# Attention in a fused four-layer kernel: Q and K normalised by two operations, the heads of Q transposed while K is made

## The reference

```
q = (layernorm(x) @ Wq).reshape(B, Sq, H, D)      # H = 16 heads, D = 128
k = (ctx @ Wk).reshape(B, Skv, H, D)
v = (ctx @ Wv).reshape(B, Skv, H, D)
q = q * rsqrt(mean(q*q, axis=-1) + eps) * gq      # per token and head
k = k * rsqrt(mean(k*k, axis=-1) + eps) * gk
attn = softmax(einsum('bqhd,bkhd->bhqk', q, k) / sqrt(D))
x = x + einsum('bhqk,bkhd->bqhd', attn, v).reshape(B, Sq, H*D) @ Wo
```

## Time and profile before

| | us |
|---|---|
| runs | 832.14, 829.62, 832.06 |
| median | 832.06 |
| the profiled execution | 832.21 |
| its span (first to last instruction) | 830.3 |
| attention's first and last step, about | 311 to 604 |

### The profile page before, as it was taken

The page is one execution under the profiler, slowest core; times in us unless marked ns, Lnnn a source line. Parts: engine busy times, 40 slices in busy tenths (PEclk is TensorE's granted clock), DMA queues, the critical chain, the costliest instruction groups (busy, mean ns, idle before and its releaser), DMA issues. The chain is left out here.

```text
span 830.3 us, 12112 instructions
## 1 busy us (share of the span) xinstructions
PE 758.1 (91%) x4322; PEld 624.7 (75%) x4322; DVE 544.8 (66%) x930; ACT 432.4 (52%) x879; POOL 383.8 (46%) x311
## 2 busy tenths in 40 slices
PE   7566766999999989999999999999799999999997
PEld 2222222888888878889889898888678888888886
DVE  6999998743433567878888887887865333333333
ACT  3876652334433346666676676667553433333432
POOL 0699874336755543223322322332233655555552
PEclk9699999999999999999999999999999999999999
DMA  4613000111446101101101020000000434342431
GB/s 138 255 52 139 19 19 1 39 39 34 143 141 195 42 1 39 39 1 40 37 3 39 2 77 1 2 1 20 20 20 22 159 100 124 93 129 91 132 96 51
DMA packets 23262, 53.88 MB, mean 65 GB/s; under 512 B 4057, under 2 KB 6690, under 8 KB 22178
## 3 DMA queue, kind: packets, MB, share of 16 engines
q1 hardware_dynamic: 23040, 52.96, 20.0%
q10 hardware_dynamic: 162, 0.14, 0.0%
HBM read 51.87 MB, written 1.21 MB: 64 GB/s over the span
## 5 line engine op out<-in xcount | busy, mean ns | idle before, releaser
L1163 POOL TENSOR_TENSOR f_h_lo<-f_hid,f_h_hi 128x512 fp32r<-128x512 f32 x84 | 108.8, 1295 | 128.2 <-ACT f_h_hi L1138 127.7
L1254 DVE TENSOR_TENSOR f_su<-f_sg,psum 128x512 f32<-128x512 f32 x72 | 49.5, 687 | 168.4 <-PE psum L111 150.9
L1138 ACT ACTIVATE f_h_hi<-f_hid 128x512 fp32r<-128x512 f32 x84 | 53.1, 632 | 164.0 <-DVE f_hid L1271 145.2
L109 PE MATMUL psum<-xT_hi,w_ring 128*128 128x512 f32 x336 | 133.8, 398 | 1.9 <-ACT f_cT L1129 0.7
L110 PE MATMUL psum<-xT_lo,w_ring 128*128 128x512 f32 x336 | 132.9, 396 | 0.0
L111 PE MATMUL psum<-xT_hi,w_ring 128*128 128x512 f32 x336 | 132.8, 395 | 0.0
L109 PE MATMUL psum<-w_ring,f_h_hi 128*128 128x256 f32 x336 | 95.3, 284 | 1.9 <-POOL f_h_lo L1163 1.2
L1657 POOL TENSOR_TENSOR a_rr<-a_ss,eps 128x8 f32<-128x8 f32 x32 | 6.5, 203 | 194.1 <-DVE a_ss L1696 194.1
L111 PE MATMUL psum<-w_ring,f_h_lo 128*128 128x256 f32 x336 | 94.5, 281 | 0.0
L110 PE MATMUL psum<-w_ring,f_h_hi 128*128 128x256 f32 x336 | 94.2, 280 | 0.0
L1568 ACT ACTIVATE a_p_exp<-psum,a_nmax 128x256 f32<-128x256 f32 x128 | 59.5, 470 | 57.5 <-DVE a_nmax L1711 57.5
(11 more groups left out here) (217 smaller groups left out, 1852.6 us busy)
## 6 DMA issues: line engine op xcount, KB each, us to landing
w_raw<-in_moe SPq DMA_DIRECT2D x42, 384.0 KB, 3.3
m_b_all<-b_rows SPq DMA_DIRECT2D x8, 1024.0 KB, 4.6
f_comb<-scratch SPq DMA_DIRECT2D x60, 128.0 KB, 3.4
a_raw<-in_w_pair SPq DMA_DIRECT2D x8, 768.0 KB, 4.3
f_comb<-scratch SPq DMA_DIRECT2D x12, 224.0 KB, 3.5
f_comb<-scratch SPq DMA_DIRECT2D x12, 192.0 KB, 3.6
f_comb<-scratch SPq DMA_DIRECT2D x12, 160.0 KB, 3.4
f_comb<-scratch SPq DMA_DIRECT2D x12, 96.0 KB, 3.5
```

What stands on the lines that cost most here:

```text
L109: pe.matmul(out, a[0], b[0], start=first, stop=False, skip_group_check=True)
L1138: act.activation(h_hi[:, j % HS, :], hid[:, j % HS, :], ACT.Copy).then_inc(mix.h_hi_s, 1)
L1163: pool.tensor_tensor(h_lo[:, j % HS, :], hid[:, j % HS, :], h_hi[:, j % HS, :], ALU.subtract)\
```

## The change

`normed` becomes two DVE operations of 512 columns each, Q first and then K, and each raises `qkn_s`. `heads_turned` waits ahead of the four transposes of Q for the first and ahead of those of K for the second. The waits that stood ahead of the calls go, and POOL's wait on the same semaphore counts in twos. The amount of work is the same.

```diff
                 def heads_turned(n):
 
                     for which, dst in enumerate((QT, KT)):
+                        pe.wait_ge(qkn_s, 2 * n + which + 1)
                         for hh in range(HP):
                             for tile in range(2):
...
                     if not (static and t >= NUA - 1):
-                        pe.wait_ge(qkn_s, t + 2)
                         heads_turned(n + 1)
...
                     norm_turned(pe, sh, s, 1, h, out)
-                pe.wait_ge(qkn_s, 1)
                 heads_turned(0)
...
                     if not (isinstance(t, int) and t < 2):
-                        pool.wait_ge(qkn_s, t - 1)
+                        pool.wait_ge(qkn_s, 2 * (t - 1))
                     pool.tensor_tensor(rr[:, n % 2, :], ss[:, n % 2, :], sh.eps[:, :], ALU.add).then_inc(mse_s, 1)
...
-                    dve.tensor_tensor(qkn[:, n % 2, :].rearrange("p (a f) -> p a f", f=HD),
-                                      qk_banks(t).rearrange("p (a f) -> p a f", f=HD),
-                                      rr[:, n % 2, :].unsqueeze(2).to_broadcast([P, 8, HD]), ALU.mult).then_inc(qkn_s, 1)
+                    for at in range(2):
+                        dve.tensor_tensor(qkn[:, n % 2, at * UW:(at + 1) * UW].rearrange("p (a f) -> p a f", f=HD),
+                                          qk_banks(t)[:, at * UW:(at + 1) * UW].rearrange("p (a f) -> p a f", f=HD),
+                                          rr[:, n % 2, 4 * at:4 * at + 4].unsqueeze(2).to_broadcast([P, 4, HD]), ALU.mult)\
+                            .then_inc(qkn_s, 1)
```

## The result

| | before | after |
|---|---|---|
| runs, us | 832.14, 829.62, 832.06, 832.50 | 826.12, 824.65, 824.31, 823.06 |
| median, us | 832.10 | 824.48 |
| ratio (95% interval) | | 0.9911 (0.9891 to 0.9931) |
| profiled execution, us | 832.21 | 826.12 |
| its span, us | 830.3 | 824.2 |

What follows compares the result with a forecast made beforehand. The prediction took the ring, 8.95 us per step, to bound the kernel. Its terms, 7.3 + 0.4 - 0.1 = 7.6 us of gain, gave 824.5 us (chance 0.80), range 821 to 828.5.

Steps and rivals of the forecast that it cites:

- the ring: Attention loop from projection through squares, sums, roots, `normed` and transposes to the next projection; 8.95 us, sets the step.
- The two halves: In `normed`: Q ready at R + 0.74, K at R + 1.34; before, both at R + 1.28.
- R: Start of `normed` in a step, the zero point from which times in us are counted.
- The transposes: PE hands over to the projection at R + 1.80, before R + 2.13: 0.33 us saved, step 8.62.
- Where it counts: Of 23 stalls in the attention, 22 gain 0.33 us each, 7.3 us; the last has no projection behind it.
- The first unit: Start of the attention, transposes partly at the low clock: 0.4 us of gain, bounds 0 and 0.7.
- The last unit: End of the attention, where the 0.06 us of longer `normed` shows: 0.1 us of loss.
- the fold steps: Seven attention steps in which PE also folds weights; PE comes to K's transposes after K is ready: no gain.
- What stands behind: Behind the longer `normed`: ACT keeps 0.23 us of cover ahead of `squares`, DVE 0.8 us idle ahead of the sums.
- other wait: Rival: another wait in the attention takes the place, leaving 3.3 us of gain, 829 us; chance 0.10.
- the halves weren't dear: Denies the rival that `normed` halves cost more: at 1.02 us each, a slower kernel, 841 us; chance 0.04.
- the clock: Rival: more PE work falls into the second low-clock stretch, in the router's products: 826.2 or 827.9 us; chance 0.06.

Runs made afterwards that it cites:

- one wait: The changed kernel, but the transposes of Q wait for both `normed` operations; ratio 1.0035 to the kernel before.
- K in two parts: The changed kernel with K's half of `normed` split again by token tile, K's transposes waiting tile by tile; ratio 0.9864 to the kernel before.
- the second profile: The changed kernel measured once more with no further edit; ratio 0.9913 to the kernel before.

## Why the prediction was right

*What bounds the kernel.* Right: the ring. It was shortened (the change), lengthened by 0.15 us on GpSimd and shortened by 0.07 us on VectorE, and the step followed by 0.38, 0.16 and 0.07 us.

*The two halves.* 681 ns each and 0.60 apart, as taken from the low parts of the probabilities: the spread operand costs nothing in four blocks either. K was there at R + 1.34, as worked out. The fixed price that the Trainium skill (VectorE: DVE Perf Modes, section on the TRN2 errata) gives would have made it 0.125 us later than the whole, not 0.06; here the measurement decides. That each operation has a price is right in kind: by itself the split made the kernel slower. The section's advice, though, is tiles of 512 elements or more, and both halves are that; it speaks against this split less than the prediction has it.

*The transposes.* Q's start was right. The hand-over was at R + 1.75, not R + 1.80: four transposes and the restart take 0.41 us, not 0.46. The restart's price, read from eight transposes that wait once, is hardly paid a second time. That made the step 8.57 instead of 8.62, and the gain of a step 0.38 instead of 0.33 us.

*Where it counts.* Twenty-two steps were too many by two. The steps behind the first unit took 8.93 and 8.84 us instead of 8.94 and 8.94, a gain of 0.1 together and not 0.7. In the first of them the sums of squares start 0.46 us behind the squares' end instead of 0.12 (0.48 with one wait, so PE's waiting between the halves isn't the reason; 0.11 with K in two parts); why, is open. So the steps gave 20 x 0.38 + 0.1 = 7.7 us where 7.3 stood in the sum: two errors against each other.

*The first unit.* 0.5 us (8.40 instead of 8.90 from `normed` to the projection), predicted 0.4; the second profile gives 0.4 (8.50). K's four transposes ran at the low clock, as expected (K ready at 308.90 + 1.34 = 310.24, the granted clock 0.53 from 310.06):

```profile
309.64 1.97 PE L1424 MATMUL psum<-ident,a_qkn 128*128 128x128 f32 x8 [0.48 <-DVE a_qkn L1705]
```

*The last unit and the fold steps.* The turning of the last probabilities comes 581.71 - 571.33 = 10.38 us behind the last projection instead of 10.32: the 0.1 us of loss. The fold steps kept their length, 9.27 instead of 9.29 us.

*What stands behind.* ScalarE's idle time ahead of the squares went from 0.62 to 0.17 us, worked out 0.23; VectorE's ahead of the sums from 1.21 to 0.79, worked out 0.8. Neither took over.

*The rivals.* No other wait took the place (the list of waits above); the halves weren't dear; the clock moved nothing behind the attention, since what follows it is as long as before to 0.04 us (0.4 us longer in the second profile). That such a thing happens is shown by other runs, though: with K in two parts the granted clock was 0.83 in the first 20 us behind the attention, and what follows took 244.2 us instead of 242.5. So this rival wasn't far-fetched; it just didn't come. The start of the kernel mattered too, 2.0 us in the profiled execution, where the prediction had only the scatter of three runs to go by. That the medians lie 7.6 us apart, exactly as predicted, is in part luck: in the attention it was 8.1 us, with two errors in the sum against each other.

## What to carry to other kernels

Where an engine waits once in each step, look for the ring behind the wait: what is saved on it comes back in each step, up to the engine's own work, and what is saved beside it nowhere. A split pays if the waiting engine can begin on the first part, and by no more than the work that it does in between; alone it costs. Giving the waiting engine other work until the second part is there takes the wait away altogether. With each wait that goes, look for the next engine that frees something, here a PSUM bank: VectorE had 0.1 us to spare for it in the changed kernel and none with K in two parts.

## What the runs showed of the hardware

- A VectorE operation starts 0.10 us behind its releaser where the engine has stood idle for 0.8 to 1.2 us, and 0.03 us behind it where another operation has ended just before (0.09 us before the releaser); operations without use put ahead of the wait made the step 0.07 us shorter.
- A small GpSimd operation (8 columns, 0.20 us shown) whose successor waits for nothing holds it up by 0.15 us; where a semaphore stands between two such operations it is 0.28 us.
- A second VectorE operation of 512 columns out of PSUM, straight behind the first, starts 0.60 us behind it, though each is shown with 0.68 us: 1024 columns in two are ready 0.06 us later than in one.
